# Giving the first chunk a lead of six inner tiles and a new written-out order to the first three chunks

## The reference

```python
x = L0_attn_x                                  # (4, 1024, 512)
x = x + _layernorm(attn(_layernorm(x), W_qkv, W_out))
x = x + _layernorm(ffn(_layernorm(x), w_gate_up, w_proj))
# attn: 16 heads of 32, all elementwise in the head
q, k = elu(q) + 1, elu(k) + 1
out = q * cumsum(k * v, axis=2) / (q * cumsum(k, axis=2) + 1e-9)
return out @ W_out.T * 32 ** -0.5
# ffn: 512 -> 2 x 2048 -> 512, its weights made ternary first
gate, up = split(x @ ternary_quant(w_gate_up).T)     # scale = mean |w| of each 64, q = clip(round(w / scale), -1, 1)
hn = rms_norm(silu(gate) * up)
return hn @ ternary_quant(w_proj).T
```

## Time and profile before

| | us |
|---|---|
| median of 3 runs | 1218.29 (1218.2 to 1219.13) |
| the profiled execution | 1217.17 |
| its span | 1215.1 |
| PE busy | 1110.6 (91%) |
| DVE busy | 791.3 (65%) |
| POOL busy | 528.3 (43%) |
| ACT busy | 441.0 (36%) |
| mean granted TensorE clock | 0.963 of full |

### The profile page before, as it was taken

One profiled execution on the slowest core, in us unless ns is written; L12 is line 12 of the kernel. 1 busy time (PEld: TensorE's weight loads), 2 busy tenths in 40 slices (PEclk: granted clock), 3 DMA queues, 4 the chain that ended last, 5 costly groups with the idle time before them and its releaser, 6 DMA issues. The chain is left out here.

```text
span 1215.1 us, 14590 instructions
## 1 busy us (share of the span) xinstructions
PE 1110.6 (91%) x5376; PEld 661.0 (54%) x5376; DVE 791.3 (65%) x1224; ACT 441.0 (36%) x752; POOL 528.3 (43%) x493
## 2 busy tenths in 40 slices
PE   6995187989989999999999999999999999899997
PEld 5774154544536676445854486446844585454443
DVE  5997757999845848843886268744885278525423
ACT  4232225656522212442234323441344313433432
POOL 1545447788643415441542434342544253215322
PEclk9997587999989999999999999999999999999999
DMA  7021013211003020000210020000200020100000
GB/s 268 1 70 35 24 63 122 87 53 45 1 0 105 1 70 36 1 1 1 70 35 1 1 70 35 1 1 9 93 3 1 1 70 1 35 1 1 35 1 35
DMA packets 29079, 44.97 MB, mean 37 GB/s; under 512 B 1361, under 2 KB 9553, under 8 KB 29009
## 3 DMA queue, kind: packets, MB, share of 16 engines
q1 hardware_dynamic: 29008, 44.05, 11.1%
HBM read 34.60 MB, written 9.44 MB: 36 GB/s over the span
## 5 line engine op out<-in xcount | busy, mean ns | idle before, releaser
L523 PE MATMUL bank<-x3t,wgu_t 128*128 128x512 f16 x1536 | 354.8, 384 | 11.3 <-ACT ht L941 7.6
L1176 POOL TENSOR_TENSOR acc<-acc,ht 128x512 f32<-128x512 f32 x105 | 136.9, 1304 | 276.0 <-ACT ht L975 275.9
L523 PEld LDWEIGHTS bank<-x3t,wgu_t 128*128 128x128 bf16 x1536 | 149.4, 99 | 195.4 <-issue 13.3
L559 PE MATMUL bank<-wproj_t,hid 128*128 128x512 bf16 x896 | 210.3, 380 | 0.0
L1448 DVE TENSOR_TENSOR ht<-ht,bank 128x512 f32<-128x512 f32 x112 | 76.1, 680 | 162.8 <-PE bank L523 128.2
L504 PE MATMUL bank<-xnt,wqkv_hi 128*128 128x512 f32 x672 | 168.7, 393 | 5.8 <-issue 2.7
L1454 DVE TENSOR_TENSOR hid<-ht,hid 128x512 f16<-128x512 f32 x112 | 98.2, 877 | 71.7 <-ACT hid L965 71.6
L559 PEld LDWEIGHTS bank<-wproj_t,hid 128*128 128x128 f16 x896 | 87.7, 98 | 103.5 <-issue 1.5
L504 PEld LDWEIGHTS bank<-xnt,wqkv_hi 128*128 128x128 f32 x672 | 125.7, 189 | 33.0 <-issue 5.7
L965 ACT ACTIVATE hid<-ht 128x512 f16<-128x512 f32 x112 | 70.5, 630 | 186.9 <-DVE ht L1448 175.0
L1118 POOL TENSOR_TENSOR tk<-tq,ts 128x512 f32<-128x512 f32 x28 | 56.4, 2015 | 140.6 <-DVE ts L1376 140.6
(11 more groups left out here) (161 smaller groups left out, 1532.6 us busy)
## 6 DMA issues: line engine op xcount, KB each, us to landing
raw_q<-in_L_ffn_w_gate_up_dram SPq DMA_DIRECT2D x32, 256.0 KB, 2.8
xn<-in_L_attn_x_dram SPq DMA_DIRECT2D x7, 1024.0 KB, 5.1
out_dram<-xn SPq DMA_DIRECT2D x7, 1024.0 KB, 8.6
x<-in_L_attn_x_dram SPq DMA_DIRECT2D x6, 1024.0 KB, 6.6
raw_q<-in_L_ffn_w_proj_dram SPq DMA_DIRECT2D x16, 256.0 KB, 3.0
raw_a<-in_L_attn_W_qkv_dram SPq DMA_DIRECT2D x4, 768.0 KB, 8.4
xn<-in_L_attn_x_dram SPq DMA_DIRECT2D x4, 256.0 KB, 3.5
raw_out<-in_L_attn_W_out_dram SPq DMA_DIRECT2D x1, 1024.0 KB, 12.5
```

What stands on the lines that cost most here:

```text
L523: last = pe.matmul(bank[:], wgu_t[:, k, first_row:first_row + P], x[:, part, k], start=(n == 0), stop=(n == 2 * KD - 1))
L559: last = pe.matmul(bank[:], hid_of(f, part, k)[:, t * P:(t + 1) * P], wproj_t[:, k], start=(k == 0 and part == 0), stop=(k == MT - 1 and p ...
L1176: pool.tensor_tensor(acc[:], acc[:], ht_of(f)[:, m % 2], ALU.add).then_inc(q["acc_done"], 1)
```

## The change

The constant BEHIND goes from 4 to 6: chunk 0 leads chunk 1 by six inner tiles. Three hidden tiles of chunk 0 get a place of their own (`hid_early`, and `acc_early` for its running sum of squares), in the memory of `outt` beside two of the weight batches, so that they need only chunk 0's `project_att` (`out_done` of 4). The helpers are cut into single operations (`scale_sums`, `scale_max`, `scale_rec`, `clip`, `round_off`, `feature_q`, `sum_keys`, `den_product`, `stats_tile` and so on), and `start()` of each of the four compute engines is one list of them in a new order. The operations are those of before, with the same shapes and numbers of instructions, but for waits; those that are new are in the diff below. `run_steps` stays as it was. The DMA queue issues `raw_a` 3 and `raw_out` behind the load of chunk 1, and its waits stand behind other half loads. Chunk 3's turning is put between the last `project_second`, and its third `group` behind `project_att` of chunk 2.

```diff
-    BEHIND = 4
+    BEHIND = 6
+    EARLY = 3
...
+        hid_early = [sb(f"hid_early{m}", [P, 2, N], FP16, at_outt + 4 * N * m) for m in range(EARLY)]
+        acc_early = sb("acc_early", [P, N], F32, at_outt + 4 * N * EARLY)
...
-            for i in range(KD + 1):
-                load_raw(i)
-            load_halves(0, RAW)
+            load_raw(0)
+            load_raw(1)
+            load_raw(2)
             sp.wait_ge(t1_done, KD)
             sp.dma_start(xn[:], x_ch[1]).then_inc(x_loaded, 16)
+            load_raw(3)
+            load_raw(4)
+            load_halves(0, 3)
...
+                    if b == 0 and i == 0:
+                        pe.wait_ge(ln2_x, NT)
+                    elif b == 1 and i == 0:
+                        pe.wait_ge(x3t_hi, KD)
+                        pe.wait_ge(x3t_lo, KD)
...
# TensorE
+                group_at(1, 0, 1, 2, 3, 4, 5, 6), project_att_at(0, 0, 1, 2, 3), group_at(1, 7, 8, 9, 10), transpose_half(0, 0, 1)
+                transpose_x1_at(0, 0, 1, 2, 3), group_at(1, 11), transpose_half(1, 0), up_unit(0, 0), transpose_half(1, 1)
+                gate_unit(0, 0), transpose_half(2, 0, 1), gate_unit(0, 1), up_unit(0, 1), gate_unit(0, 2), transpose_half(3, 0, 1)
+                up_unit(0, 2), gate_unit(0, 3), up_unit(0, 3), project_att_at(1, 0, 1, 2, 3), transpose_half(4, 0, 1)
+                transpose_half(5, 0, 1), gate_unit(0, 4), transpose_half(6, 0), up_unit(0, 4), transpose_half(6, 1)
...
+                transpose_half(23, 0), gate_unit(1, 9), transpose_half(23, 1), up_unit(1, 9), gate_unit(1, 10), up_unit(1, 10)
+                transpose_x_at(2, 0), gate_unit(1, 11), project_first(14, 15), transpose_x_at(2, 1), up_unit(1, 11), square_sums_at(0)
+                gate_unit(1, 12), transpose_x_at(2, 2), up_unit(1, 12), gate_unit(1, 13), transpose_x_at(2, 3), up_unit(1, 13)
+                gate_unit(1, 14), up_unit(1, 14), gate_unit(1, 15), up_unit(1, 15), group_at(2, 0, 1, 2), square_sums_at(1)
+                group_at(2, 3, 4, 5), project_second(0, 1, 2, 3, 4, 5), group_at(2, 6, 7, 8), project_second(6, 7), group_at(2, 9, 10, 11)
+                project_second(8, 9, 10, 11, 12, 13), transpose_x_at(3, 0, 1), project_second(14), transpose_x_at(3, 2, 3)
+                project_second(15), group_at(3, 0, 1), project_att_at(2, 0, 1, 2, 3), group_at(3, 2)
...
# ScalarE
                     if m == MT // 2:
-                        act.wait_ge(out_done, NT)
+                        act.wait_ge(FF_MAIN["pr_done"], EARLY)
+                    if m == MT // 2 + EARLY:
+                        act.wait_ge(ss_done, 1)
...
                     if f == 0 and m == 0:
+                        act.wait_ge(out_done, NT)
+                    if f == 0 and m == EARLY:
                         act.wait_ge(out_done, 2 * NT)
...
+                cast_half(4, 0, 1), turn(0, 1), put_half(0, 0), cast_half(5, 0, 1), out_hi(1, 1), put_half(0, 1)
+                x3_hi_of(0, 0, 1, 2), feature_relu(1, 3, 0), feature_exp(1, 3, 0), x3_hi_of(0, 3), feature_relu(1, 3, 1)
...
# GpSimd
+                pool.wait_ge(kv_done, at(KD, s, j))
                 pool.tensor_tensor(tk[:, d], tq[:, d], ts[:, d], ALU.mult).then_inc(den_mul, 1)
...
+                rstd_bias("3", 0), norm_x1_tile(0, 0, 1, 2, 3), divide(2), power_lead(1), power_rest(1), power_take(1)
+                den_product(1, 2), den_guard(1, 2), scale_back(2), num_product(1, 2), divide(3, 4, 5), scale_back(3)
+                den_product(1, 3), den_guard(1, 3), num_product(1, 3), scale_back(4), divide(6), power_lead(2), power_rest(2)
+                power_take(2), add_square(0, 1), scale_back(5), divide(7), scale_back(6), divide(8, 9), add_square(0, 2)
...
# VectorE
+                add_ln2_tile(0, 0, 1, 2, 3), row_shrink(0), round_off(1), stats_tile("3", 0, 0, 1), feature_k(1, 2)
+                stats_tile("3", 0, 2, 3), stats_join("3", 0, 0, 1), scale_max(2), stats_join("3", 0, 2, 3), scale_rec(2)
+                stats_mean("3", 0), stats_var("3", 0), scale_row(2), feature_q(1, 2), scale_sums(3), diff(0), back_reciprocal(1, 1)
+                scale_max(3), front_products(1, 2), scale_row(3), scale_rec(3), scale_bound(1), scale_sums(4), clip(2)
+                back_output(1, 1), diff(1), round_off(2), sum_keys(1, 2), back_lo(1, 1), x3_lo_of(0, 0, 1, 2, 3), row_shrink(1)
+                scale_max(4), scale_sums(5), feature_k(1, 3), sum_values(1, 2), diff(2), scale_rec(4), scale_max(5), carry_key(1, 2)
+                carry_value(1, 2), scale_rec(5), scale_sums(6, 7), hidden_value(0, 0), back_reciprocal(1, 2), clip(3)
+                feature_q(1, 3), clip(4), round_off(3), hidden_lo(0, 0), front_products(1, 3), hidden_value(0, 1), sum_keys(1, 3)
+                sum_values(1, 3), diff(3), round_off(4), carry_key(1, 3), carry_value(1, 3), scale_row(4), scale_max(6)
+                scale_rec(6), scale_row(5), scale_bound(2), clip(5), scale_max(7), scale_rec(7), back_reciprocal(1, 3)
+                back_output(1, 2), back_output(1, 3), back_lo(1, 2), hidden_lo(0, 1), back_lo(1, 3), round_off(5), clip(6)
```

More of the change, by code:

```diff
@@ L189, in sandwich_kernel @@
         TURNED = {0: [2], 1: [3], 2: [4], 3: [5]}
-        for m in range(BEHIND, MT):
+        for m in range(4, MT):
             n = TURNED[m - 1][-1] + 1
@@ L450, in _, with transpose_raw @@
         def _(pe):
-            def transpose_raw(first, last):
-                for r, bank, _, _, _ in weight_tiles(first, last):
+            def transpose_raw(*tiles):
+                for r in tiles:
+                    (_, bank, _, _, _), = weight_tiles(r, r + 1)
                     i, n = divmod(r, 3) if r < NG else (KD, r - NG)
@@ L584, in project, with project_first, project_second, gate_unit @@
                 last.then_inc(q["pr_done"], 1)
-            def project_second(k):
-                wait_hid(1, k)
-                for t in range(NT):
-                    last = project_tile(1, k, t)
-                last.then_inc(FF_SECOND["pr_done"], 1)
+            def project_first(*tiles):
+                for k in tiles:
+                    project(0, k)
+            def project_second(*tiles):
+                for k in tiles:
+                    if k == 0:
+                        pe.wait_ge(FF_SECOND["silu_done"], MT)
+                        pe.wait_ge(FF_SECOND["h_done"], MT)
+                        pe.wait_ge(ss_read, 2)
+                    wait_hid(1, k)
+                    for t in range(NT):
+                        last = project_tile(1, k, t)
+                    last.then_inc(FF_SECOND["pr_done"], 1)
+            def gate_unit(f, m):
+                unit(f, m, 0)
+            def up_unit(f, m):
+                unit(f, m, 1)
             def square_sums(f):
@@ L838, in _, with split_weight, cast_half @@
         def _(act):
-            def split_weights(first, last):
-                for r, bank, hi, _, cols in weight_tiles(first, last):
+            def split_weight(*tiles):
+                for i in tiles:
+                    (r, bank, hi, _, cols), = weight_tiles(i, i + 1)
                     act.wait_ge(wa_t, r + 1)
                     act.activation(hi[:, :, cols], bank[:].rearrange("p (k n) -> p k n", k=KD), ACT.Copy).then_inc(wa_hi, 1)
-            def cast(b):
+            def cast_half(b, *halves):
@@ L877, in turn @@
+            def turn(*tiles):
+                for m in tiles:
                     act.wait_ge(q_shrink, m // 2 + 1)
@@ L1085, in row_power, with power_take @@
+            def power_take(i):
                 pool.wait_ge(q_power, 2 * i + 2)
[L1086 to L1095 removed]
+                pool.tensor_tensor(power_of(i), power_of(i), shrink[:, 2 * i:2 * i + 2], ALU.subtract).then_inc(q_grow, 1)
@@ L1248, in _, with split_weight @@
         def _(dve):
-            def split_weights(first, last):
-                for r, bank, hi, lo, cols in weight_tiles(first, last):
+            def split_weight(*tiles):
+                for i in tiles:
+                    (r, bank, hi, lo, cols), = weight_tiles(i, i + 1)
                     dve.wait_ge(wa_hi, r + 1)
@@ new lines, in round_off, with diff @@
+            def round_off(*batches):
+                for b in batches:
+                    y = PLACES[b][1][:]
+                    dve.wait_ge(q_clip, b + 1)
+                    dve.tensor_scalar(y, y, ROUND, ROUND, ALU.add, ALU.subtract).then_inc(q_tern, 1)
+            def diff(*batches):
+                for b in batches:
+                    wb, yq = PLACES[b]
+                    dve.wait_ge(q_wh, b + 1)
+                    dve.tensor_tensor(yq[:], yq[:], wb[:], ALU.subtract).then_inc(q_diff, 1)
@@ L1320, in stats, with stats_join @@
+            def stats_join(which, c, *tiles):
+                q = LN[which]
+                for t in tiles:
                     dve.wait_ge(q["stats_s"], 2 * NT * c + (t + 1))
@@ new lines, in add_ln2_tile, with x3_lo_of @@
+            def add_ln2_tile(f, *tiles):
+                for t in tiles:
+                    if t == 0:
```

(7 more changed lines are left out.)

865 lines of the change are left out of this document (442 added, 423 removed).

## The result

| | before | after |
|---|---|---|
| median of the comparison, us | 1218.24 (1216.69 to 1219.13) | 1158.89 (1158.54 to 1160.26) |
| ratio | | 0.9516, 95% interval 0.95 to 0.9533 |
| span of the profiled execution, us | 1215.1 | 1158.4 |
| mean granted TensorE clock | 0.963 | 0.984 |

A forecast was written before the change was run, and what follows sets the result against it. VectorE's late `x3t` starved TensorE in `start()` from 105 to 143 us; then VectorE and GpSimd set the pace. Gains of 31 + 4.5 + 4.5 = 40, less 1 us for loads, gave 1179 us, range 1163 to 1199.

The forecast's parts named there:

- up to `scale_back(5)`: From the kernel's start to GpSimd's `scale_back(5)`: it would start at 149.5 us instead of 180.27.
- the tail: From the last transposed half to chunk 2's first group: 31 us instead of 35.58, 4.5 us earlier.
- chunk 2's attention and chunk 3's start: Interleaved turning of chunk 3 and its third group behind `project_att(2)`: 4.5 us more gain, bound at 0 and 5.
- the loads: Later loads of `raw_a` 3 and `raw_out`: at worst 2 us, of which 1 us was taken off the gain.
- To the last transposed half: From `scale_back(5)` at the old VectorE and GpSimd rate, 149.2 us: last half at 299 us, 31 us earlier.
- The prediction's check: TensorE from 149 us to the last half: some 129 us of work, end 278, so it doesn't bind.
- My bound of 288: Time of the last transposed half if VectorE and GpSimd ran with no wait: 288 us, against 299 forecast.
- To `x3t` and `project_att(1)`: `add_ln2(0)` at 94 us, `x3t` ready at 118 instead of 142, `project_att(1)` at 149 instead of 158.23.
- The first (the port takes more): Rival: VectorE and GpSimd's shared port costs the stretch 8% more (12 us); about 1197 us, chance 0.20.
- The second: Rival: the hole only moves, and only VectorE's idle from 105 to 143 us is won; 1207 us, chance 0.06.
- third: Rival: TensorE waits at transposed halves hold everything; above 2.2 us a batch the lead is gone; 1223 us at 2.5, chance 0.05.
- more than it: Whole kernel: a gain beyond the forecast, time below 1167 us, chance 0.07.

The follow-up runs named there:

- Experiment 1: Kernel before, from inner tile 4 on VectorE clips and rounds the next batch ahead of `diff`: 1235.5 us, ratio 1.0147.
- Experiments 2: Kernel before without the 30 `add_square` additions of chunks 0 and 1 on GpSimd: 1201.22 us, 17 less.
- 3: Changed kernel without the 30 `add_square` additions of chunks 0 and 1 on GpSimd: 1158.02 us, 0.9 less.
- 7: Changed kernel with 64 TensorE matmuls (low half of hidden values) left out of chunk 0's feed-forward projection: 1151.79 us, 7.1 less.
- 8: Kernel before with the low half's 64 TensorE matmuls left out of chunk 0's feed-forward projection: 1215.72 us against 1217.74.
- 11: Changed kernel with two TensorE waits removed by order (`up_unit(0, 15)`, `row_shrink(2)` and `turn(4, 5)` earlier): 1155.31 us, ratio 0.9486.
- Experiment 4: Changed kernel with `x3_lo(0)`, sums of batches 6 and 7 and first two hidden values back behind chunk 1's last sums: 1176.05 us, 17.2 more.
- 9: Kernel before with only chunk 0's `x3` pieces early, on VectorE and ScalarE: 1218.2 us, ratio 1.0006.
- 12: Kernel before with only VectorE's rounding one batch earlier around chunk 1's attention projection: 1219.8 us, ratio 1.0021.
- 13: Kernel before with rounding earlier on VectorE, and GpSimd taking `divide(6)` and `scale_back(5)` ahead of chunk 1's norm: 1215.56 us, ratio 0.9979.
- 10: Kernel before with only TensorE's new order of chunk 3's start: 1210.28 us, ratio 0.9939.

## Why the prediction was right in its direction and short in its size

The gain beyond the forecast is 17.7 us by the spans. By the prediction's own steps:

| step | short by, us |
|---|---|
| up to `scale_back(5)` (forecast 149.5, came at 143.6) | 5.9 |
| from there to the last transposed half | 6.8 |
| the tail | 2.8 |
| chunk 2's attention and chunk 3's start | -0.9 |
| `run_steps` | 2.1 |
| the loads | 1 |

**The step that failed** is "To the last transposed half": "I keep the rate", because of the 7.6 us of excluded parts "nothing in it is left to squeeze". The stretch took 142.9 us, not 149.2. That is 6.3 us; the 6.8 of the table has 0.5 more because 31 stood for 31.5. Counted by batches, `scale_back(5)` to (9) took 38.2 us before and 33.5 after; from (9) to (23) the rate went from 7.39 to 6.93 us a batch, which is 6.4 us over 14 batches; and from the last `scale_back` to the last half it took 4.0 us longer, 12.3 instead of 8.3. The sum of parts that exclude one another had come out above the cycle itself (7.6 against 6.86), and I took this for a full cycle. But it counted GpSimd's parts and VectorE's in one row, while a `diff` that is held by GpSimd is held beside work that GpSimd has to do anyway; and the gaps of 2.03 and 1.42 us in the earlier trace rows were in sight: GpSimd waiting for the rounding. Experiment 1 shows that the order alone moves the cycle, 6.86 to 8.3 us. The changed order moves the rate the other way, with 10.7 us of such waits instead of 28.4. The two groups of `diff` from 204 us on before and from 200 us on after:

```profile
L1311 DVE TENSOR_TENSOR yq<-yq,wb 128x1024 bf16<-128x1024 bf16 x17 | 29.7, 1747 | 0.9 <-POOL yq L1093 0.9
```

```profile
L1396 DVE TENSOR_TENSOR yq<-yq,wb 128x1024 bf16<-128x1024 bf16 x11 | 10.6, 963 | 2.9 <-POOL yq L1114 2.9
```

A `diff` takes 963 ns in the mean instead of 1747. The prediction had named a longer `diff` as a sign against it; it went the other way, and that was a second thing not foreseen. But neither fewer waits for the rounding nor a short `diff` explains the gain by itself, since experiment 1 had both (11.2 us and 680 ns) and was slower. What goes with the length of the stretch in all three kernels is VectorE's busy time over nearly the same number of instructions: 153.96 us in a stretch of 171.3 us (experiment 1), 132.71 in 149.9 (before), 116.75 in 142.9 (after). Which entries of the new order made the difference is open. The Trainium skill (SBUF — State Buffer, "SBUF: two separate sides") has the two engines block each other for whole instructions, and single rows here agree, as that `diff` of 2.17 us in the earlier trace rows. How many of them meet is set by the order, as these three busy times show.

**Which engine sets the time.** The prediction's check had TensorE free to end the stretch at 278 and therefore not binding. That was right for the 299 I forecast and wrong for what came: 286.5 us, with TensorE busy 134.39 us of the 144.58 from `project_att(1)` on. Experiments 2, 3, 7 and 8 together show the exchange, and 11 that TensorE's single waits count now. My bound of 288 for "VectorE and GpSimd with no wait" was passed, because it started from 149.5 and the stretch began at 143.6.

**To `x3t` and `project_att(1)`.** The path was right, the waits on it too large: `add_ln2(0)` was 1 us better than forecast, from there to the end of `x3_lo(0)` it took 21.3 us where 21.4 and 2.5 for holding were counted, and the 4 us of waits before `back_lo(1, 3)` were one idle gap of 0.33 us. The granted clock was below full there too, 0.78 in that stage against 0.54 from 105 to 143 us before, but VectorE, which had its own work of chunk 1 to do, did not have to wait for TensorE.

**What carries the lead.** Experiment 4 shows that the early `x3t` is worth 17 us in the new order, 9 that it is worth nothing in the old one, where ScalarE's half copies stayed behind attention's output; 12 and 13 show the same of the rounding (+2 and -2.6 us). The parts that I could try alone in the kernel before (0 in 9, 7.5 in 10, 2.6 in 13) sum to 10 us of 59. In 9, 12 and 13 the removed wait was taken over by the next entry in another engine's list. The rest of the gain is not assigned to parts: it belongs to the four lists together. Of the change I did not try BEHIND at 4 in the new order, nor the early hidden tiles by themselves.

**The tail.** Forecast 31 us with 2 us of waiting, measured 28.28 with none. The late norm of chunk 2 had gone under the row of units wholly. The slow restart at 431.18 was priced against the wrong rows: eight matmuls of that form take 1.98 us at full clock, not the 1.75 of a `project`. Two groups took 7.14 us there instead of 5.44, so that with the wait of 2.05 some 3.75 us were to be had. The start of chunk 3 had been put at 4.5 us; it gave 3.6 to the start of `run_steps` and 2.1 within it, where I had expected no change. In the waits of TensorE behind 450 us, the one for `x3t` goes from 3.1 to 1.5 us and one of 1.0 us for `x` is gone, which may be because the work that stands ahead of them on VectorE is done earlier; no run separates it.

**The rivals.** The first (the port takes more) has the sign of the effect wrong: VectorE's busy time in the stretch fell by 16 us, and GpSimd's rose by 5.6. The second and third did not come: the waits of TensorE at the halves are 18.5 us in 11 over the whole stretch of 24 batches, 0.8 us a batch, below the 2.2 at which the third would have decided. What I forecast at 0.07, "more than it", came true. All my bounds on the good side were taken from work that stays as dense as it was; none allowed for a rate that improves.

## What to carry to other kernels

When two engines hand work to each other in a cycle, sum the idle gaps before each hand-over before calling the cycle full. Such gaps say that an engine isn't full; whether another order wins them has to be measured, for experiment 1 cut one kind from 28.4 to 11.2 us and lost 18 us. Judge an order by the busy time of both engines over the whole stretch, and not by the length of one operation. And try a reordering as a whole: a wait taken out of one list goes to the next entry of the partner's list, so that a part worth nothing alone (experiment 9) can be worth 17 us with the rest (experiment 4).

## What the runs showed of the hardware

The only thing that I had not expected is how much of the holding between VectorE and GpSimd depends on who starts first. In experiment 1 a `diff` that starts at 244.12 us, 0.16 us ahead of a `scale_back`, takes its 0.68 us and the `scale_back` 2.28 instead of 1.90; the `diff` of the earlier trace rows that starts 0.29 us behind a divide takes 2.17 us. GpSimd's own operations stretch as well: `scale_back` takes 1890 to 2342 ns in the changed kernel, and its mean is 2052 ns where it was 1928, while VectorE's `diff` fell from 1513 to 1025 ns over the kernel. Over the stretch from `scale_back(5)` to the last half GpSimd's busy time rises from 116.18 to 121.74 us (19 `scale_back` and 17 divides in both, three additions fewer after; the mean divide goes from 1912 to 2185 ns), and VectorE's falls from 132.71 to 116.75:

```profile
180.27:330.20 149.93, 135.16 (x822) 69.84 (x820) 132.71 (x204) 86.34 (x159) 116.18 (x84) 0.93 0.20 62
```

```profile
143.62:286.51 142.89, 132.70 (x834) 73.52 (x833) 116.75 (x206) 81.57 (x150) 121.74 (x89) 0.96 0.22 70
```

The groups of the two operations, before and after:

```profile
L1093 POOL TENSOR_TENSOR yq<-yq,gsc 128x1024 bf16<-128x1024 bf16 x24 | 46.3, 1928 | 53.6 <-DVE yq L1303 53.6
L1311 DVE TENSOR_TENSOR yq<-yq,wb 128x1024 bf16<-128x1024 bf16 x24 | 36.3, 1513 | 0.9 <-POOL yq L1093 0.9
```

```profile
L1114 POOL TENSOR_TENSOR yq<-yq,gsc 128x1024 bf16<-128x1024 bf16 x24 | 49.2, 2052 | 12.6 <-DVE yq L1389 12.5
L1396 DVE TENSOR_TENSOR yq<-yq,wb 128x1024 bf16<-128x1024 bf16 x24 | 24.5, 1025 | 2.9 <-POOL yq L1114 2.9
```
